# Two of four key chunks as fp16 halves, with the weight splits moved to the start: a graph-attention layer with a feed-forward layer

## What is computed

```python
q = (x @ Wq).reshape(N, HEADS, DH); k = ...; v = ...        # x: normalised rows
scores = jnp.einsum('nhd,mhd->hnm', q * SCALE, k)
scores = jnp.where(adj[None, :, :] > 0, scores, NEG_INF)
attn = jax.nn.softmax(scores, axis=-1)
sat = jnp.einsum('hnm,mhd->nhd', attn, v).reshape(N, V_DIM)
out = jnp.concatenate([sat[:SIZE_U] @ weightr, sat[SIZE_U:] @ weightd], axis=0)
x = x + jax.nn.leaky_relu(out + bias, negative_slope=0.01)
...
h = jax.nn.gelu(jnp.einsum('td,edh->teh', xf, W1) + b1[None], approximate=False)
y = jnp.einsum('teh,ehd->ted', h, W2) + b2[None]
x = x + jnp.einsum('ted,te->td', y, mf)                     # mf: the 2 best of 8 experts
```

## Time and profile before

| | |
|---|---|
| three runs | 812.86, 813.87, 814.46 us |
| profiled execution | 814.02 us, span 811.8 us |
| TensorE busy | 786.7 us, 97% |
| VectorE busy | 644.9 us, 79% |
| ScalarE busy | 683.9 us, 84% |
| GpSimd busy | 475.5 us, 59% |
| DMA | 45.08 MB, 56 GB/s on average |

### The profile page before, as it was taken

How to read it: one execution, slowest core, us unless ns; L and a number is a source line. 1 busy time by engine, 2 the same in 40 slices (tenths; PEclk the granted TensorE clock), 3 DMA queues, 4 the chain that set the end, 5 groups by cost and what they waited for, 6 DMA issues and landing times.

```text
span 811.8 us, 33322 instructions
## 1 busy us (share of the span) xinstructions
PE 786.7 (97%) x12576; PEld 586.4 (72%) x12576; DVE 644.9 (79%) x1469; ACT 683.9 (84%) x1099; POOL 475.5 (59%) x490
## 2 busy tenths in 40 slices
PE   3989999999999999999999999999999999999997
PEld 2367777777777777777777777777777667777775
DVE  6788898888989898888889888888975767555554
ACT  4678898888888898888888888888887999999996
POOL 4167473847466464747556474746631767676764
PEclk9999999999999999999999999999999999999999
DMA  9634434433343344333443443334200000000000
GB/s 227 118 60 70 77 61 68 87 59 58 59 76 66 58 69 74 64 58 58 68 74 58 64 83 60 58 58 73 43 0 2 2 15 15 15 13 13 13 13 13
DMA packets 40909, 45.08 MB, mean 56 GB/s; under 512 B 22168, under 2 KB 32160, under 8 KB 40864
## 3 DMA queue, kind: packets, MB, share of 16 engines
q0 software_dynamic: 9216, 33.56, 25.8%
q1 hardware_dynamic: 31216, 10.71, 5.7%
q10 hardware_dynamic: 432, 0.20, 0.1%
HBM read 71.72 MB, written 2.10 MB: 91 GB/s over the span
## 4 chain that ended last, share of the span: by engine, by line
PE 93%; ACT 2%; DVE 2%; issue 1%; DMA 1%; POOL 0%; DVEq 0%; ACTq 0%
PE ps L1095 22%; PE ps L1043 20%; PE ps L1064 19%; PE ps L1089 6%; PE ps L1217 4%; PE ps L1218 3%; PE ps L1219 3%; PE ps L1196 3%; PE ps L1197 3%; PE ps L1198 3%; PE ps L1106 2%; PE ps L995 1%; PE ps L1003 1%; PE ps L1013 1%; PE ps L1114 1%
## 5 line engine op out<-in xcount | busy, mean ns | idle before, releaser
L710 DVE CUSTOM_DVE_ANT_0 prob<-ps,mask 128x1024 f32<-128x1024 f32 x256 | 311.5, 1221 | 37.0 <-PE ps L1043 30.7
L517 ACT ACTIVATE prob<-prob,nmax 128x1024 f32<-128x1024 f32 x256 | 293.0, 1145 | 0.0
L1064 PEld LDWEIGHTS ps<-ident,prob 64*128 64x128 f32 x4096 | 152.6, 138 | 61.5 <-issue 58.7
L1043 PE MATMUL ps<-k_half,q_row 64*128 64x512 f16 x1536 | 187.6, 376 | 1.9 <-DVE k_half L665 1.5
L1095 PE MATMUL ps<-pt,v_sb 128*64 128x128 f32 x3072 | 189.1, 276 | 0.2 <-issue 0.2
L1064 PE MATMUL ps<-ident,prob 64*128 64x64 f32 x4096 | 180.3, 227 | 4.5 <-ACT prob L517 1.5
L1095 PEld LDWEIGHTS ps<-pt,v_sb 128*64 128x64 f32 x3072 | 165.9, 137 | 6.9 <-issue 0.6
L444 POOL TENSOR_TENSOR prob<-prob 128x512 f16<-128x512 f32 x104 | 124.1, 1196 | 63.6 <-ACT prob L595 60.5
L342 POOL TENSOR_TENSOR pt_lo<-pt_raw,pt_hi 128x1024 f16<-128x1024 f32 x62 | 134.5, 2170 | 5.2
L537 ACT ACTIVATE pt<-ps 128x1024 f32<-128x1024 f32 x96 | 98.4, 1025 | 43.6 <-PE ps L1064 43.4
L339 POOL TENSOR_SCALAR pt_hi<-pt_raw 128x1024 f16<-128x1024 f32 x62 | 77.2, 1245 | 83.7 <-ACT pt_raw L537 69.0
(11 more groups left out here) (124 smaller groups left out, 1079.3 us busy)
## 6 DMA issues: line engine op xcount, KB each, us to landing
mask<-in_adj POOLq DMA_DIRECT2D x64, 512.0 KB, 5.5
q_row<-q_nat SPq DMA_DIRECT2D x128, 32.0 KB, 4.7
x_sb<-in_x SPq DMA_DIRECT2D x4, 512.0 KB, 7.0
out<-x_sb SPq DMA_DIRECT2D x8, 256.0 KB, 2.3
x2t_hi<-in_L_ffn_W SPq DMA_DIRECT2D x1, 1024.0 KB, 6.5
wq_sb<-in_L_gnn_Wq ACTq DMA_DIRECT2D x1, 64.0 KB, 2.9
wk_sb<-in_L_gnn_Wk ACTq DMA_DIRECT2D x1, 64.0 KB, 4.4
...
```

What stands on the lines that cost most here:

```text
L517: act.activation(prob[:, h, cols], prob[:, h, cols], ACT.Exp, bias=nmax[:, h:h + 1], scale=-1.0, accum_out=sums[:, j, h, p:p + 1]).then_in ...
L710: dve.tensor_tensor_reduce(out=prob[:, h, col_of(p)], in0=ps[:, 2 * (u % 2):2 * (u % 2) + 2, :].rearrange("p b c -> p (b c)"), in1=mask[:, ...
L1043: ins = pe.matmul(ps[:, 2 * (u % 2) + half, :], q_row[part, par, h, a, :], k_half[part, h, b, cols], start=first, stop=final)
L1064: ins = pe.transpose(ps[:, bank + half, t * DH:(t + 1) * DH], prob[part, h, (p * KT + t) * P:(p * KT + t + 1) * P], ident[part, part])
```

## The change

1. **A second chunk as halves.** `SPLIT_P` is (1, 3) and `SPLIT_UNITS` (1, 3, 5, 7), so GpSimd splits four units of a tile and TensorE takes chunk 3 as halves too, but for tile 31. `pt_raw` keeps two buffers, unit 5 follows unit 1 in the one and 7 follows 3 in the other; the copies of a unit wait for the split of the one before it. `pt_lo` is made by two instructions of 512 columns. The halves lie in `pt_half`, where `xn_t` lies before (so the first splits wait for `project_v`), and the low and high values of chunk 3 in the place of the raw values of chunk 1.
2. **GpSimd's step** has splits 5 and 7 behind the first DMA issue, and inverse deviation and normalisation between them.
3. **The feed-forward weights** are split in four parts of 512 columns ahead of the loop, after VectorE's last `normalise_x`; the adjacency of tile 2 is loaded between and behind them. The small weights follow between splits 5 and 7 of tile 0, the value halves of chunk 3 behind split 7 of tile 0.
4. **Orders at the start and the end.** The inverse deviations of x are made in runs of 4, 4, 8, 8, 8 tiles, VectorE's row statistics are cut in two functions and interleaved, the first scores wait for fewer k halves, in step 1 the transposes go ahead of `project_v` in two blocks, and at the end the first `up` goes ahead of the last chunk of tile 31.

The diff, cut:

```diff
-SPLIT_P = 1
-SPLIT_UNITS = (1, 3)
-WHOLE = (0, 2, 4, 5, 6, 7)
+SPLIT_P = (1, 3)
+SPLIT_UNITS = (1, 3, 5, 7)
+NS = len(SPLIT_UNITS)
+WHOLE = (0, 2, 4, 6)
...
-        pt_hi = sb("pt_hi", [P, 2, KT, P], F16)
-        pt_lo = sb("pt_lo", [P, 2, KT, P], F16)
+        pt_half = sb("pt_half", [P, 2, NS, KT, P], F16)
...
+        v_first = sb("v_first", [P, 2, KT, D], F16)
+        v_later = v_sb[:, KT:2 * KT, :].rearrange("p t d -> p (t d)").bitcast(F16).rearrange("p (m t d) -> p m t d", m=2, t=KT)
+        v_pair = (v_first, v_later)
...
+        SMALL_SPLITS, PART_SPLITS, W_PARTS = 8, 6, 4
+        W_PART = E * H // W_PARTS
...
+            def split_values(n):
+
+                p = SPLIT_P[n]
+                raw = v_sb[:, p * KT:(p + 1) * KT, :]
+                pool.wait_ge(v_ready, 2 * p + 2)
+                if n > 0:
+                    pool.wait_ge(v_lo_ready, n)
+                pool.tensor_scalar(v_pair[n][:, 0, :, :], raw, 1.0, 0.0, ALU.mult, ALU.add).then_inc(v_hi_ready, 1)
+                pool.wait_ge(v_hi_ready, n + 1)
+                pool.tensor_tensor(v_pair[n][:, 1, :, :], raw, v_pair[n][:, 0, :, :], ALU.subtract).then_inc(v_lo_ready, 1)
 
...
-                if not early:
-                    pool.wait_ge(av_done, NP * j + SPLIT_P - 3)
+                if early:
+                    pool.wait_ge(v_psum, V_FIRST + q + 1)
+                else:
+                    pool.wait_ge(av_done, NP * j + UNITS[u][1] - 3)
                 pool.nop(nofuse=True)
-                pool.tensor_scalar(pt_hi[:, q, :, :], pt_raw[:, q, :, :], 1.0, 0.0, ALU.mult,
+                pool.tensor_scalar(pt_hi[:, q, :, :], pt_raw[:, q % 2, :, :], 1.0, 0.0, ALU.mult,
                                    ALU.add).then_inc(pt_hi_by_pool, 1)
-                pool.wait_ge(pt_hi_by_pool, 2 * j + q + 1)
-                pool.tensor_tensor(pt_lo[:, q, :, :], pt_raw[:, q, :, :], pt_hi[:, q, :, :],
-                                   ALU.subtract).then_inc(pt_by_pool, 1)
-
-            def inverse_std_x(i):
-
-                part = slice(i * X_TILES, (i + 1) * X_TILES)
-                pool.wait_ge(var_ready, i + 1)
+                pool.wait_ge(pt_hi_by_pool, NS * j + q + 1)
+                for part in (slice(0, KT // 2), slice(KT // 2, KT)):
+                    ins = pool.tensor_tensor(pt_lo[:, q, part, :], pt_raw[:, q % 2, part, :], pt_hi[:, q, part, :],
+                                             ALU.subtract)
+                ins.then_inc(pt_by_pool, 1)
...
+            def split_ffn_part(n):
+
+                part = slice(n * W_PART, (n + 1) * W_PART)
+                split_weights(w_split_chain, PART_SPLITS * n, w1_raw[:, part], w1_pair[:, :, part])
+                split_weights(w_split_chain, PART_SPLITS * n + 3, w2_raw[:, part], w2_pair[:, :, part])
...
+            def step(i, par, post=True, load=True, early=False, last=False):
+
+                split_pt(i - 1, 1, early)
                 if post and par == 0:
                     residual(i - 4)
-                if prior:
-                    split_pt(i - 1, 3, early)
+                split_pt(i - 1, 3, early)
                 if load:
                     load_adj(i + 2, par, 0)
-                if split and par == 0:
-                    split_ffn_part(i)
+                if not last:
+                    split_pt(i - 1, 5, early)
+                if early:
+                    split_small()
                 if post and par == 0:
                     inverse_std(i - 4)
                     normalise(i - 4)
+                if not last:
+                    split_pt(i - 1, 7, early)
                 if load:
                     load_adj(i + 2, par, 1)
...
-            step(0, 0, prior=False, post=False, split=False)
-            split_values()
             pool.wait_ge(w1_in, 16)
             pool.wait_ge(w2_in, 16)
-            split_ffn_part(0)
-            pool.wait_ge(w_in, 16 * N_W)
-            split_weights(6, wg_sb[:, :], wg_pair)
-            split_weights(9, b2_sb[:, :], b2_pair)
-            pool.tensor_scalar(ident16[:, :], ident[:, :], 1.0, 0.0, ALU.mult, ALU.add).then_inc(w_split_chain, 1)
-            pool.tensor_scalar(wrd[:, :, :, :], wrd[:, :, :, :], 1.0 / V_UP, 0.0, ALU.mult, ALU.add).then_inc(w_split_chain, 1)
+            pool.wait_ge(xn_by_dve, NC)
+            for n in range(W_PARTS - 1):
+                split_ffn_part(n)
+            load_adj(2, 0, 0)
+            split_ffn_part(W_PARTS - 1)
+            load_adj(2, 0, 1)
+            split_values(0)
             step(1, 1, post=False, early=True)
+            split_values(1)
             step(2, 0, post=False)
             step(3, 1)
             pairs(pool, 4, NT - 2, step)
             step(NT - 2, 0, load=False)
             step(NT - 1, 1, load=False)
-            step(NT, 0, prior=False, load=False, split=False)
+            step(NT, 0, load=False, last=True)
...
-                    if not early:
-                        act.wait_ge(pt_by_pool, 2 * j + u // 2 - 1)
-                    to = pt_raw[:, u // 2, :, :]
+                    if not early or u > 4:
+                        act.wait_ge(pt_by_pool, NS * j + u // 2 - 1)
+                    to = pt_raw[:, u // 2 % 2, :, :]
...
-                if p == SPLIT_P and not whole:
-                    pe.wait_ge(pt_by_pool, 2 * j + 2)
+                if p in SPLIT_P and not whole:
+                    pe.wait_ge(pt_by_pool, NS * j + p + 1)
...
-                    if early:
+                    if early and k >= AV_BLOCK:
                         project_v(V_FIRST + k)
                     if prior:
                         transposes(i - 1, 2 * k + 1, early, not now)
+                    if early and k < AV_BLOCK:
+                        project_v(V_FIRST + k)
...
+            pe.wait_ge(pt_by_act, NU * NT)
+            pe.wait_ge(pt_by_dve, copies_by_dve(NT, 0))
+            pe.wait_ge(w_split_chain, PART_SPLITS * W_PARTS)
+            up(0, 0, 0, early=True)
+            attend(NT - 1, NP - 1, whole=True)
+            logits(NT - 2 * PAIR)
```

136 lines of the change are left out of this document (70 added, 66 removed).

## The result

The kernel after takes 818.21 us (median of four runs, 817.22 to 818.62) against 814.0 for the kernel before in the same comparison (812.86 to 814.46): a ratio of 1.005, 95% interval 1.0038 to 1.0062. It is slower by 4.2 us; the forecast was 805.1. The profiled execution took 818.53 us with a span of 816.9 (before: 811.8). The four executions are not alike in TensorE's mean granted clock: two have 0.993 and spans of 816.9 and 816.5, two have 0.996 and spans of 815.1 and 814.9; only one of the first kind was profiled.

A forecast was written before the change was run, and what follows sets the result against it. The prediction took TensorE's list of work, busy 97% of the span, as the bound. Its terms, -12.8 + 4.8 - 0.9 = -8.9, took 814.0 to 805.1 us, with a range from 800 to 815.5.

The forecast's parts named there:

- Term 1: TensorE in the attention loop: a second halved chunk saves 0.44 us per tile, for 29 tiles -12.8 us.
- Term 2: GpSimd in the loop: needs 34.6 us of a 35.2 us pair, so it keeps up and the full 0.44 stays.
- Rival B: Loop: TensorE waits about 0.4 us per pair for a late split 7 or late mask; 810.9 us, chance 0.17.
- Term 3: Start: weight splits on GpSimd delay chunk 3's low values to 79.6, so TensorE waits: +4.8 us.
- Term 4: End: halved chunk 1 of the last step -0.44, earlier first gelu saves half of a 0.97 wait; together -0.9 us.
- rival D: Loop: new halves do not run at the old halves' rate, only start and end remain; 817.9 us, chance 0.03.

The follow-up runs named there:

- d_stat: Kernel after with small weight splits behind the value halves, the end's old order, and statistics before the even step's second mask: 807.12 us.
- d_norm: Kernel after with small weight splits behind the value halves, the end's old order, and GpSimd's inverse deviation and normalisation before split 5: 806.73 us.
- f_fill: Kernel after, with 24 unused matmuls on TensorE while it waits for the value halves of chunk 3 of tile 0: 817.03 us.
- f_inv: Kernel after with small weights behind value halves, normalisation before split 5, earlier weight splits, last two tiles' inverse deviation and normalisation one expert later: 803.49 us.

## Why the prediction was wrong

**Term 1 (0.44 us per tile, -12.8) was right.** The halved chunk 3 takes 1.46 us to the next instruction's start, and with the late mask gone the pair lasts 35.22 to 35.24 in five kernels, against 36.10: 0.88 for two tiles.

**Term 2 failed in its last two sentences, not in its sum.** GpSimd fits, as forecast, with 33.1 us of a pair where 34.6 were reckoned; it has idle time in every pair. The step that failed is: "VectorE's own waits, up to 1.1 us at two masks of a pair, fall where it idles (31.5 of 35.2 busy)". The size was right, 1.09 us at one mask. The place was wrong: 3.7 us of idle time in a pair is a mean, and at the second mask of the even step statistics, a score and a copy for TensorE stand in an unbroken row. That costs 0.45 us a pair. Rival B had both the mechanism and the price (0.4 a pair), and I gave it 0.17 on the ground of that mean. d_stat and d_norm, two different edits that both shorten this mask, get the time back: 35.22 for 35.65. The Trainium skill's lock (SBUF — State Buffer, section "SBUF: two separate sides") was cited for the wait; the trace agrees with it as to the length (1.09 us more, behind a pt_hi of 1.06), and the kernel's order alone said where it falls.

**Term 3 had its own number right and stopped there.** The value halves came at 80.05 (79.6 forecast) and TensorE rested 5.46 us. Missing was what a rest costs beyond itself: 2.6 us at half clock (f_fill), a cost put at nothing without a reason. The steps of before have no rest over 1.2 us that could show it, but its first rows do: behind TensorE's 11.64 us of rest at the very start the same four matmuls take nearly twice as long as 7 us later (the view gives the clock as 1.00 there).

```profile
14.35 3.75 PE L995 MATMUL ps<-pt,wq_sb 128*128 128x512 f32 x4 [0.78 <-ACT pt L471]
...
21.34 1.98 PE L995 MATMUL ps<-pt,wq_sb 128*128 128x512 f32 x4
```

The other missing item is the wait of 1.52 us at 140.41.

**Term 4 had the wrong sign.** I held that the normalisation of the last two tiles "comes a little later than now" and left it there. It is what GpSimd's in-order queue waits for, with four low halves for TensorE behind it: +2.6 instead of -0.9 by the spans, of which 1.0 is the longer wait, 1.7 the clock behind it and 0.3 a wait for the gates (636.25), less the 0.44 for chunk 1. That -0.44 was right (24.61 against 25.05), the -0.5 from an earlier first gelu did not come: with the queue mended (f_inv), the early up is worth nothing.

**The sum.** By the spans the forecast missed 14.0 us (+5.1 against -8.9): 4.9 up to the second output projection (clock 2.6, the "issue" wait 1.5, 0.5 because the value halves were used at 80.13 and not 79.6, 0.3 without a name), 5.6 in the steps behind it (the late mask) and 3.5 at the end. Each of these alone would have stayed under the range's end of 815.5; that they could come together was left out. The measured time lies next to rival D's 817.9, and that is luck: D's mechanism, halves that do not run at the old rate, is not there.
